# ScalarE takes the logarithms first, an affine step behind each, in the fractal stage of a four-layer kernel

## Chip, cores, metric

One core of a Trainium2 chip. The metric is the time of one launch on the device in microseconds. TensorE (PE in the profile, its weight loads PEld), VectorE (DVE), ScalarE (ACT), GpSimd (POOL) and SyncE (SP), which here issues DMAs, each run a queue of their own in order, and wait for one another through semaphores.

## What is computed

x has shape (16, 224, 224, 32) in fp32. Four layers follow each other, each of the form `x = x + f(group_norm(x))`; the change touches the first of them, the fractal layer:

```python
def _L0_conv_ref(x, gamma, beta, moving_mean, moving_var):
    x = sample_min_max_scaling(x)                       # (x - min) / (max - min + 1e-7), by sample
    measures = jnp.stack([box_sum(x, r) for r in (2, 4, 8, 16)], axis=-1)
    log_scales = jnp.log(jnp.asarray(SCALES))
    log_measures = jnp.log(measures + 1e-7)
    dls = log_scales - mean(log_scales)
    alphas = sum((log_measures - mean(log_measures)) * dls) / sum(dls ** 2)
    return (alphas - moving_mean) / jnp.sqrt(moving_var + 1e-3) * gamma + beta
x = x + _L0_conv_ref(_gn(x), ...)
```

box_sum(x, r) sums each channel over r x r pixels, stride 1, same size. The slope alpha of four logarithms is a fixed combination of them; with the batch-norm constants it becomes one scale and one bias for each channel. The other three layers (two spectral ones and a 7 x 7 convolution) are not touched.

## The kernel before

The program runs its layers as passes, one after the other, a barrier between them: `pass_fractal`, `mix_modes`, `pass_spectral`, `pass_conv`, `mix_modes`, `pass_inverse`. The change lies in `pass_fractal`, the first 3.6 ms. It goes through B = 16 samples. A sample has UN = 16 steps u: eight groups of four channels (cg) by two overlapping tiles of 128 rows (t). A step's tile is 128 rows by 224 columns by 4 channels.

What happens to step u of sample s, by engine:

- ScalarE `scale` (L350) applies the sample's normalisation and min-max scaling, from X into H0, in two halves. For u = 0 it waits for the sample's coefficients (`coef_ready`, from L673 on VectorE).
- VectorE `sums` (L526, L531, L534) adds H0 with itself shifted, in three levels, into Hb: sums over 2, 4 and 8 columns. The third sets h_ready, which frees H0 and starts the boxes.
- TensorE `boxes` (L429) multiplies these with band matrices: the sums over rows. It does so in four parts j, two for each half of the columns, each part with two PSUM banks. Parts 0 and 2 share their banks, as do 1 and 3, so part j waits for the logarithm of part j - 2 (ln_done), and sets m_ready.
- ScalarE `logs` (L361) takes the logarithm of each part, from PSUM into L (L[:, u % 2], four slots, one for each scale).
- VectorE `combine` (L541, L543) makes the slope out of the four slots, in L's slot 0 (t_ready). It waits for all four logarithms.
- ScalarE `affine` (L369) applies scale and bias, one instruction for each channel, from slot 0 into slot 2 of L (z_ready).
- VectorE `add` (L551) adds x and slot 2 into the compact buffer X1[:, u % 4] (x1_ready). It also waits until the buffer is free: the row matmuls (zps_ready) and the put-back (x_back) of four steps before.
- ScalarE `put_back` (L376) copies X1 into X, so that whole rows can be stored (x_back). VectorE `stats_of_x1` (L558) takes its group statistics. TensorE `over_rows` (L440) and `over_columns` (L451) transform X1 for the next layer, and ScalarE `keep_rows_done` (L381) moves the rows' result out of PSUM.

The order on each engine is written out by hand in its `body(prev, cur, nxt)`, which goes over the sixteen steps of one sample and mixes in what is left of the sample before and what prepares the next. For an ordinary step u:

- VectorE: sums(u+1) with stats_of_x1(u-2) between the levels, combine(u), add(u-1). In steps 4 to 10 then two or three pieces of statistics and extremes of the next sample (`stats_of_x`, L572 and L574), in step 11 their fold, in steps 3, 5, 6 and 12 to 14 small operations that make coefficients.
- ScalarE: scale(u+1), [keep_rows of prev in steps 1 and 2], put_back(u-2), [keep_rows in odd steps from 5], logs(u), affine(u-1). In step 15 it is scale of the next sample's step 0.
- TensorE: boxes(u), small matmuls of the statistics, [over_columns in steps 0, 3, 8, 12], over_rows. Step 1 has two over_rows, step 2 none.
- SyncE `finish`: when the last put-back of a sample is done (in ScalarE's step 1 of the next one), it stores the sample from X in two halves (L283), and when a half is stored it loads the same half of the sample after next into its place (L277). VectorE's first stats_of_x, in step 4, waits for the first half.

Two samples stand in one turn of a hardware loop (`Fori`); the first sample and the last are written out beside it.

Of the kernel before, what the change touches and what calls it, by code (L numbers as in the profile page):

```python
# [21 lines left out]
ALU = mybir.AluOpType  # L22
ACT = mybir.ActivationFunctionType
# [3 lines left out]
W = 224  # L27
# [7 lines left out]
HALF = W // 2  # L35
CG = 4
NCG = C // CG
# [40 lines left out]
def after(engine, sem, count):  # L78

    if not isinstance(count, int) or count > 0:  # L80
        engine.wait_ge(sem, count)
# [119 lines left out]
def pass_fractal(nc, B, d, keep):  # L201

    UN = NCG * T
    with Scope(nc, "a_") as z:
        X = z.sb("X", [P, 2, T, W, C])
        H0 = z.sb("H0", [P, WP, CG])
        Hb = z.sb("H", [P, 2, 3, WP, CG])
        L = z.sb("L", [P, 2, len(SCALES), W, CG])
        X1 = z.sb("X1", [P, 4, W, CG])
# [9 lines left out]
        eps = z.sb("eps", [P, 1])  # L219
        par4 = z.sb("par4", [P, 4, C])  # L220
        alp = z.sb("alp", [P, 2, C])
# [12 lines left out]
        PS = z.ps("PS", [P, 8, 512])  # L234
# [6 lines left out]
        sem = {n: z.sem(n) for n in names}  # L241
# [4 lines left out]
        def U(s, u):  # L246
            return s.e * UN + u
# [7 lines left out]
        def looped(engine, body, steps=None, per_turn=0):  # L255
            n = turns(body)
            with engine.Fori(0, n) as i:
                if steps:
                    steps.enter(i, per_turn)
                body(Sample(i, 0), Sample(i, 1), Sample(i, 2))  # L260
                body(Sample(i, 1), Sample(i, 2), Sample(i, 3))
            if steps:
                steps.leave(n)
            body(Sample(n, 0), Sample(n, 1), None)
            body(Sample(n, 1), None, None)
# [73 lines left out]
        @block.scalar  # L339
        def _(act):  # L340
            def scale(s, u):
                cg, t = divmod(u, T)
                if u == 0:
                    after(act, sem["coef_ready"], s.e + 1)
                    for j in range(T):
                        after(act, x_in[s.par][j], s.use * 16 + 16)
                after(act, sem["h_ready"], U(s, u))
                for k in range(0, CG, 2):
                    c = cg * CG + k
                    last = act.activation(H0[:, PAD:PAD + W, k:k + 2], X[:, s.par, t, :, c:c + 2], ACT.Relu,  # L350
                                          scale=cf[:, s.par, 0, c:c + 1], bias=cf[:, s.par, 1, c:c + 1])
                last.then_inc(sem["xs_ready"], 1)

            def logs(s, u):
                after(act, sem["x1_ready"], U(s, u) - 1)
                for j in range(4):
                    yh, sp_ = divmod(j, 2)
                    after(act, sem["m_ready"], U(s, u) * 4 + (j + 1))
                    out = L[:, u % 2, 2 * sp_:2 * sp_ + 2, HALF * yh:HALF * yh + HALF, :].rearrange("p s y c -> p s (y c)")
                    b0 = 2 * (j % 2)  # L360
                    act.activation(out, PS[:, b0:b0 + 2, 0:2 * W], ACT.Ln, bias=eps[:, 0:1])\  # L361
                       .then_inc(sem["ln_done"], 1)

            def affine(s, u):
                cg = u // T
                after(act, sem["t_ready"], U(s, u) + 1)
                for k in range(CG):
                    c = cg * CG + k
                    last = act.activation(L[:, u % 2, 2, :, k], L[:, u % 2, 0, :, k], ACT.Identity,  # L369
                                          scale=alp[:, 0, c:c + 1], bias=alp[:, 1, c:c + 1])  # L370
                last.then_inc(sem["z_ready"], 1)

            def put_back(s, u):
                cg, t = divmod(u, T)
                after(act, sem["x1_ready"], U(s, u) + 1)
                act.activation(X[:, s.par, t, :, cg * CG:cg * CG + CG], X1[:, u % 4], ACT.Copy)                   .then_inc(sem["x_back"], 1)  # L376

            def keep_rows_done(s, cg):
                after(act, sem["modes_ready"], s.e * 4 + (cg // 2 - 1))
                after(act, sem["zps_ready"], s.e * NCG + (cg + 1))  # L380
                act.activation(Zs[:, cg // 2 % 2, :, cg % 2, :], PS[0:YQ * CG, 4 + cg % 2, :].rearrange("p (y q) -> p y q", q=64),  # L381
                               ACT.Copy).then_inc(sem["zev_done"], 1)

            def body(prev, cur, nxt):
                for u in range(UN):
                    if u < UN - 1:
                        if cur:
                            scale(cur, u + 1)
                    elif nxt:
                        scale(nxt, 0)  # L390
                    if u == 0 and prev:
                        affine(prev, UN - 1)
                    if prev and u == 1:
                        keep_rows_done(prev, 6)
                    if prev and u == 2:
                        keep_rows_done(prev, 7)
                    if prev and u == 6:
                        after(act, sem["modes_ready"], prev.e * 4 + 4)
                        after(act, sem["modes_stored"], prev.e * 32 + 32)
                        act.activation(SO[:], PS[:, 6, :], ACT.Copy).then_inc(sem["modes_out"], 1)  # L400
                    if cur and u >= 2:
                        put_back(cur, u - 2)
                    elif prev and u < 2:
                        put_back(prev, UN - 2 + u)
                    if cur and u >= 5 and u % 2 == 1:
                        keep_rows_done(cur, (u - 5) // 2)
                    if cur:
                        logs(cur, u)
                    if u > 0 and cur:
                        affine(cur, u - 1)  # L410

            act.wait_ge(sem["setup"], 2)
            looped(act, body)

        @block.tensor
# [84 lines left out]
        def _(dve):  # L500
# [45 lines left out]
            def add(s, u):  # L546
                cg, t = divmod(u, T)
                after(dve, sem["z_ready"], U(s, u) + 1)
                after(dve, sem["zps_ready"], s.e * NCG + (u // 2 - 1))
                after(dve, sem["x_back"], U(s, u) - 3)  # L550
                dve.tensor_tensor(X1[:, u % 4], X[:, s.par, t, :, cg * CG:cg * CG + CG], L[:, u % 2, 2], ALU.add).then_inc(sem["x1_ready"], 1)  # L551

            def stats_of_x1(s, u, j):
                cg, t = divmod(u, T)
# [47 lines left out]
            def body(prev, cur, nxt):  # L602
                for u in range(UN):
# [43 lines left out]
                    if u > 0 and cur:  # L647
                        add(cur, u - 1)
                    if u == 0 and prev:
                        add(prev, UN - 1)  # L650
# [963 lines left out]
```

## Time and profile before

| | us |
|---|---|
| median of 3 runs | 8881.9 (8867.0 to 8884.9) |
| profiled execution | 8875.9 |
| its span, first to last instruction | 8874.3 |
| fractal stage within it | 0 to about 3620 |
| busy: TensorE, VectorE, ScalarE | 7419, 5668, 3869 |

The page divides the span into forty slices of 222 us; the digits are tenths. The first sixteen slices are the fractal stage, where the line of VectorE reads 7 to 8, that of TensorE 7 to 8, and that of ScalarE 6:

```profile
PE   5788777777877778579999997999999999429887
DVE  7888888888888887435544455555555554464444
ACT  4666666666666667213323332434434433101111
```

In a line of the groups, the name after the line number is the engine, then operation, what it writes and reads, shapes and count; behind the bar busy time, the mean of one in ns, and the idle time of the engine just before it with what ended it. In a timeline the first two numbers are the start in us from the span's start and the time taken; neighbours on one engine overlap by about 0.1 us, so the distance between starts is the better measure of what an instruction costs. A number in brackets is idle time just before it.

### The profile page before, as it was taken

Reading aid. Unit: us, or ns where it says so; the run is one execution under the profiler, and the core shown is the slowest. Engines: PE = TensorE matmul, PEld = TensorE weight load, DVE = VectorE, ACT = ScalarE, POOL = GpSimd, SP = SyncE. Lnnn points to the kernel's source line nnn. Section 1 sums busy time; section 2 is a strip of 40 time slices with the busy share of each in tenths; the row PEclk is TensorE's granted clock in tenths of the full one; section 3 lists DMA queues with packets and bytes.
Section 4 is the critical chain, followed back from the end, with each engine's and each line's share of the span. In section 5 each row is a group of like instructions: output and inputs, shape, how many; then the busy total and the mean of one; then the engine's idle time right before and its main releaser. Section 6 shows DMA issues by size and latency. Waiting matters only on the chain. (4 is left out here: it accounts for less than half of the span.)

```text
span 8874.3 us, 105845 instructions
## 1 busy us (share of the span) xinstructions
PE 7419.2 (84%) x34656; PEld 4519.8 (51%) x34656; DVE 5667.7 (64%) x10505; ACT 3869.1 (44%) x5030; POOL 276.2 (3%) x146
## 2 busy tenths in 40 slices
PE   5788777777877778579999997999999999429887
PEld 2444444444444444346666664566666666425444
DVE  7888888888888887435544455555555554464444
ACT  4666666666666667213323332434434433101111
POOL 0000000000000000100000000000000000000000
PEclk9989999999999999678888888999999999669998
DMA  1111111111111110644444445766766765589998
GB/s 71 64 64 64 64 64 64 64 64 64 64 64 64 64 64 31 173 115 138 150 130 136 136 136 174 180 168 167 183 166 165 181 170 150 185 300 241 262 256 237
DMA packets 780381, 1175.10 MB, mean 132 GB/s; under 512 B 154850, under 2 KB 693842, under 8 KB 759618
## 3 DMA queue, kind: packets, MB, share of 16 engines
q1 hardware_dynamic: 641858, 920.90, 34.9%
q10 hardware_dynamic: 133120, 140.54, 6.0%
q0 software_dynamic: 5120, 110.11, 3.9%
q8 instruction: 151, 2.47, 0.1%
q14 instruction: 132, 1.08, 0.0%
HBM read 706.47 MB, written 464.91 MB: 132 GB/s over the span
## 5 line engine op out<-in xcount | busy, mean ns | idle before, releaser
L429 PE MATMUL a_PS<-a_H,a_band 128*128 128x448 f32 x5120 | 2270.6, 596 | 656.1 <-ACT a_L L361 390.8
L429 PEld LDWEIGHTS a_PS<-a_H,a_band 128*128 128x128 f32 x5120 | 1027.9, 209 | 1739.1 <-issue 1146.3
L1163 PE MATMUL d_PS<-d_N,d_Bd 128*128 128x504 f32 x3072 | 1374.3, 599 | 85.6 <-ACT d_R L1270 58.1
L361 ACT ACTIVATE a_L<-a_PS,a_eps 128x896 f32<-128x896 f32 x1024 | 1007.3, 1003 | 666.1 <-PE a_PS L429 664.8
L1026 DVE SCALAR_TENSOR_TENSOR c_XO<-c_PS,c_XC 128x128 f32<-128x128 f32 x1792 | 495.9, 397 | 749.5 <-PE c_PS L948 746.1
L1163 PEld LDWEIGHTS d_PS<-d_N,d_Bd 128*128 128x128 f32 x3072 | 576.8, 193 | 739.6 <-issue 733.6
L1346 DVE TENSOR_TENSOR d_X<-d_R,d_X 128x504 f32<-128x504 f32 x512 | 348.3, 680 | 877.6 <-ACT d_R L1270 877.6
L541 DVE TENSOR_TENSOR a_L<-a_L 128x1792 f32<-128x1792 f32 x256 | 517.8, 2023 | 454.5 <-ACT a_L L361 454.5
L369 ACT ACTIVATE a_L<-a_L,a_alp 128x224 f32<-128x224 f32 x1024 | 732.6, 795 | 0.4 <-DVE a_L L543 0.4
L1469 DVE TENSOR_TENSOR e_OUT<-e_PS,e_X 112x224 f32<-112x224 f32 x1024 | 424.6, 531 | 455.7 <-PE e_PS L1424 254.3
L982 ACT ACTIVATE c_XT<-c_PS 128x512 f32<-128x512 f32 x448 | 267.5, 597 | 990.6 <-PE c_PS L937 990.5
L1270 ACT ACTIVATE d_R<-d_PS,d_b 128x504 f32<-128x504 f32 x512 | 346.7, 680 | 779.5 <-PE d_PS L1163 669.5
L948 PEld LDWEIGHTS c_PS<-c_Ws,c_XT 128*128 128x128 f32 x3584 | 457.1, 200 | 363.8 <-ACT c_XT L982 308.0
L1424 PE MATMUL e_PS<-e_V,e_G 128*112 128x448 f32 x1024 | 487.2, 604 | 85.6 <-DVE e_OUT L1469 85.6
L948 PE MATMUL c_PS<-c_Ws,c_XT 128*128 128x128 f32 x3584 | 545.5, 298 | 0.0
L1173 PEld LDWEIGHTS d_PS<-d_F,d_XP 112*112 112x112 f32 x4096 | 486.3, 184 | 96.8 <-issue 57.7
L944 PE MATMUL c_PS<-c_V,c_G 64*128 64x512 f32 x896 | 535.3, 679 | 0.2 <-DVE c_XO L1026 0.2
L1173 PE MATMUL d_PS<-d_F,d_XP 112*112 112x128 f32 x4096 | 491.4, 280 | 37.6 <-ACT d_XP L1230 37.6
L1303 DVE TENSOR_SCALAR d_N<-d_X,d_cf 128x56 f32<-128x56 f32 (+1 forms) x1536 | 482.9, 374 | 19.0 <-DMA d_X<-tmp_x 11.2
L572 DVE TENSOR_TENSOR a_run<-a_run,a_X 128x896 f32<-128x896 f32 x448 | 466.3, 1083 | 0.0
L440 PEld LDWEIGHTS a_PS<-a_F,a_X 128*112 128x112 f32 x4096 | 438.7, 180 | 51.9 <-issue 48.0
L1450 ACT ACTIVATE e_V<-e_PS 128x448 f32<-128x448 f32 x256 | 139.1, 543 | 735.4 <-PE e_PS L1415 735.4
(183 smaller groups left out, 8584.3 us busy)
## 6 DMA issues: line engine op xcount, KB each, us to landing
d_X<-tmp_x SPq DMA_DIRECT2D x512, 252.0 KB, 5.0
a_X<-in_x SPq DMA_DIRECT2D x32, 3584.0 KB, 19.0
c_XC<-tmp_x SPq DMA_DIRECT2D x448, 256.0 KB, 2.8
tmp_x<-d_X SPq DMA_DIRECT2D x512, 204.8 KB
tmp_x<-a_X SPq DMA_DIRECT2D x32, 3136.0 KB, 17.9
tmp_x<-c_XO SPq DMA_DIRECT2D x32, 3136.0 KB, 20.0
d_XR<-tmp_x ACTq DMA_DIRECT2D x256, 392.0 KB, 5.6
e_X<-tmp_x SPq DMA_DIRECT2D x256, 392.0 KB, 7.2
```

Source lines behind the costliest of these rows:

```text
L361: act.activation(out, PS[:, b0:b0 + 2, 0:2 * W], ACT.Ln, bias=eps[:, 0:1])\
L369: last = act.activation(L[:, u % 2, 2, :, k], L[:, u % 2, 0, :, k], ACT.Identity, scale=alp[:, 0, c:c + 1], bias=alp[:, 1, c:c + 1])
L429: last = pe.matmul(PS[:, 2 * (j % 2) + k, 0:2 * W], band[:, pos, :], Hb[:, u % 2, level, y1:y1 + HALF, :].rearrange("p y c -> p (y c)"), s ...
L541: steps.done(dve.tensor_tensor(lu[:, 0:2], lu[:, 0:2], lu[:, 2:4], ALU.subtract))
L572: steps.done(dve.tensor_tensor(run[:, j], first if k == 1 else run[:, j], now, op))
L944: pe.matmul(PS[:, 4 + n % 2, :], Gr[:, t, :], V[:, 16 * q:16 * q + 16, :].rearrange("a y c -> a (y c)"), start=True, stop=False)
L948: last = pe.matmul(PS[:, 4 + n % 2, j * P:j * P + P], XT[:, n % 2, j * P:j * P + P], Ws[:], start=False, stop=(j == 3))
L1026: last = dve.scalar_tensor_tensor(out=XO[:, t, ph, :, 4 * q:4 * q + 4].rearrange("p c y -> p y c"), in0=PS[:, 4 + n % 2, :].rearrange("p ( ...
L1163: last = pe.matmul(PS[:, c % 2, 0:NW], Bd[:, c * 3 + s, :], N2[:, c % 4, :, s:s + NY], start=(s == 0), stop=(s == 2))
L1173: last = pe.matmul(PS[0:HALF, 2 + 2 * (cg % 2) + yc, k * P:k * P + P], XP[:, cg % 2, k, t, 2 * yc:2 * yc + 2, :].rearrange("p k y -> p (k ...
L1303: last = dve.tensor_scalar(N2[:, c % 4, b0:b1, 1:1 + NY], X2[:, cg % 4, b0:b1, k, :], cf[:, v, 0, c:c + 1], cf[:, v, 1, c:c + 1], ALU.mult ...
L1424: last = pe.matmul(PS[0:R, 4 + 2 * (cp % 2) + t, 0:2 * W], Gr[:, t, :], V[:, cp % 4, :], start=True, stop=True)
```

## The change

In ScalarE's body the four logarithms of step u and the four affine instructions of step u-1 alternate, and stand right behind scale(u+1); keep_rows and put_back(u-2) come behind them. The affine writes into X1 in place of L's slot 2, and VectorE's add adds x to X1 in place. The waits that guard X1 (zps_ready, x_back) go from the add to the first affine, and the first logarithm waits for z_ready of two steps before (L read) where it waited for x1_ready of two steps before.

```diff
-            def logs(s, u):
-                after(act, sem["x1_ready"], U(s, u) - 1)
-                for j in range(4):
...
+            def logs(s, u, j):
+                if j == 0:
+                    after(act, sem["z_ready"], U(s, u) - 1)
+                yh, sp_ = divmod(j, 2)
+                after(act, sem["m_ready"], U(s, u) * 4 + (j + 1))
...
+            def affine(s, u, k):
                 cg = u // T
-                after(act, sem["t_ready"], U(s, u) + 1)
-                for k in range(CG):
-                    c = cg * CG + k
-                    last = act.activation(L[:, u % 2, 2, :, k], L[:, u % 2, 0, :, k], ACT.Identity,
-                                          scale=alp[:, 0, c:c + 1], bias=alp[:, 1, c:c + 1])
-                last.then_inc(sem["z_ready"], 1)
+                if k == 0:
+                    after(act, sem["t_ready"], U(s, u) + 1)
+                    after(act, sem["zps_ready"], s.e * NCG + (u // 2 - 1))
+                    after(act, sem["x_back"], U(s, u) - 3)
+                c = cg * CG + k
+                last = act.activation(X1[:, u % 4, :, k], L[:, u % 2, 0, :, k], ACT.Identity,
+                                      scale=alp[:, 0, c:c + 1], bias=alp[:, 1, c:c + 1])
+                if k == CG - 1:
+                    last.then_inc(sem["z_ready"], 1)
...
-                    if u == 0 and prev:
-                        affine(prev, UN - 1)
+                    for j in range(4):
+                        if cur:
+                            logs(cur, u, j)
+                        if u > 0 and cur:
+                            affine(cur, u - 1, j)
+                        elif u == 0 and prev:
+                            affine(prev, UN - 1, j)
...
+                    if cur and u >= 5 and u % 2 == 1:
+                        keep_rows_done(cur, (u - 5) // 2)
                     if cur and u >= 2:
                         put_back(cur, u - 2)
                     elif prev and u < 2:
                         put_back(prev, UN - 2 + u)
-                    if cur and u >= 5 and u % 2 == 1:
-                        keep_rows_done(cur, (u - 5) // 2)
-                    if cur:
-                        logs(cur, u)
-                    if u > 0 and cur:
-                        affine(cur, u - 1)
...
             def add(s, u):
                 cg, t = divmod(u, T)
                 after(dve, sem["z_ready"], U(s, u) + 1)
-                after(dve, sem["zps_ready"], s.e * NCG + (u // 2 - 1))
-                after(dve, sem["x_back"], U(s, u) - 3)
-                dve.tensor_tensor(X1[:, u % 4], X[:, s.par, t, :, cg * CG:cg * CG + CG], L[:, u % 2, 2], ALU.add).then_inc(sem["x1_ready"], 1)
+                dve.tensor_tensor(X1[:, u % 4], X1[:, u % 4], X[:, s.par, t, :, cg * CG:cg * CG + CG], ALU.add)\
+                   .then_inc(sem["x1_ready"], 1)
```

## Rows read from the trace of the kernel before

**Rows 1.** Groups by line from 0 to 3620 us, VectorE's, then ScalarE's.
```profile
L541 DVE TENSOR_TENSOR a_L<-a_L 128x1792 f32<-128x1792 f32 x256 | 517.8, 2023 | 454.5 <-ACT a_L L361 454.5
...
L543 DVE SCALAR_TENSOR_TENSOR a_L<-a_L 128x896 f32<-128x896 f32 x256 | 279.6, 1092 | 8.8
L551 DVE TENSOR_TENSOR a_X<-a_X,a_L 128x896 f32<-128x896 f32 x256 | 277.6, 1084 | 0.7 <-ACT a_L L369 0.7
...
L361 ACT ACTIVATE a_L<-a_PS,a_eps 128x896 f32<-128x896 f32 x1024 | 1007.3, 1003 | 666.1 <-PE a_PS L429 664.8 <-issue 0.2
...
L361 ACT ACT_TABLE_LOAD x1 | 1.3, 1283 | 0.0
```

**Rows 2.** VectorE's timeline: starts of L541, steps 0 to 4, 11 to 15, 0.
```profile
1422.14 2.03 DVE L541 TENSOR_TENSOR a_L<-a_L 128x1792 f32<-128x1792 f32 x1 [7.65 <-ACT a_L L361]
...
1433.33 2.03 DVE L541 TENSOR_TENSOR a_L<-a_L 128x1792 f32<-128x1792 f32 x1 [2.53 <-ACT a_L L361]
...
1444.80 2.03 DVE L541 TENSOR_TENSOR a_L<-a_L 128x1792 f32<-128x1792 f32 x1 [2.92 <-ACT a_L L361]
...
1457.38 2.02 DVE L541 TENSOR_TENSOR a_L<-a_L 128x1792 f32<-128x1792 f32 x1 [3.21 <-ACT a_L L361]
...
1468.72 2.03 DVE L541 TENSOR_TENSOR a_L<-a_L 128x1792 f32<-128x1792 f32 x1 [2.56 <-ACT a_L L361]
...
1578.02 2.01 DVE L541 TENSOR_TENSOR a_L<-a_L 128x1792 f32<-128x1792 f32 x1
...
1589.20 2.02 DVE L541 TENSOR_TENSOR a_L<-a_L 128x1792 f32<-128x1792 f32 x1 [1.43 <-ACT a_L L361]
...
1600.87 2.02 DVE L541 TENSOR_TENSOR a_L<-a_L 128x1792 f32<-128x1792 f32 x1 [0.77 <-ACT a_L L361]
...
1612.06 2.03 DVE L541 TENSOR_TENSOR a_L<-a_L 128x1792 f32<-128x1792 f32 x1 [2.33 <-ACT a_L L361]
...
1627.92 2.02 DVE L541 TENSOR_TENSOR a_L<-a_L 128x1792 f32<-128x1792 f32 x1 [4.45 <-ACT a_L L361]
...
1641.62 2.03 DVE L541 TENSOR_TENSOR a_L<-a_L 128x1792 f32<-128x1792 f32 x1 [3.11 <-ACT a_L L361]
```

**Rows 3.** ScalarE's timeline: step 2, and the scale of step 15.
```profile
1435.98 1.47 ACT L350 ACTIVATE a_H<-a_X,a_cf 128x448 f32<-128x448 f32 x2
...
1437.81 0.94 ACT L376 ACTIVATE a_X<-a_X 128x896 f32<-128x896 f32 x1
1438.65 1.89 ACT L361 ACTIVATE a_L<-a_PS,a_eps 128x896 f32<-128x896 f32 x2
...
1443.76 1.01 ACT L361 ACTIVATE a_L<-a_PS,a_eps 128x896 f32<-128x896 f32 x1 [0.50 <-PE a_PS L429]
1444.67 2.88 ACT L369 ACTIVATE a_L<-a_L,a_alp 128x224 f32<-128x224 f32 x4
...
1617.60 1.45 ACT L350 ACTIVATE a_H<-a_X,a_cf 128x448 f32<-128x448 f32 x2 [2.77 <-DVE a_cf L673]
```

**Rows 4.** TensorE's timeline: steps 0 (second half), 1 and 2.
```profile
1414.56 6.51 PE L429 MATMUL a_PS<-a_H,a_band 128*128 128x448 f32 x10 [4.34 <-ACT a_L L361]
...
1424.22 8.03 PE L429 MATMUL a_PS<-a_H,a_band 128*128 128x448 f32 x20
1432.09 3.27 PE L440 MATMUL a_PS<-a_F,a_X 128*112 128x64 f32 x32
...
1439.70 4.03 PE L429 MATMUL a_PS<-a_H,a_band 128*128 128x448 f32 x10 [0.52 <-ACT a_L L361]
```

**Rows 5.** Windows: stretch, length, busy time of each engine, granted clock, DMA share, GB/s.
```profile
1416.00:1420.00 4.00, 4.00 (x7) 1.88 (x6) 0.00 (x0) 0.56 (x1) 0.00 (x0) 0.55 0.00 0
```

**Rows 6.** SyncE's timeline, and the time to landing by DMA issue, 1400 to 1640 us.
```profile
1427.45 0.91 SPq L283 DMA_DIRECT2D tmp_x<-a_X  x2
1441.26 9.05 SPq L277 DMA_DIRECT2D a_X<-in_x  x2
...
a_X<-in_x SPq DMA_DIRECT2D x2, 3584.0 KB, 18.2
```

More of the change, by code:

```diff
@@ L352, in scale @@
                 last.then_inc(sem["xs_ready"], 1)
-            def logs(s, u):
-                after(act, sem["x1_ready"], U(s, u) - 1)
-                for j in range(4):
[L357 to L364, printed above, removed]
-                cg = u // T
-                after(act, sem["t_ready"], U(s, u) + 1)
-                for k in range(CG):
-                    c = cg * CG + k
-                    last = act.activation(L[:, u % 2, 2, :, k], L[:, u % 2, 0, :, k], ACT.Identity,
-                                          scale=alp[:, 0, c:c + 1], bias=alp[:, 1, c:c + 1])
-                last.then_inc(sem["z_ready"], 1)
+            def logs(s, u, j):
[3 more added lines that the diff above has]
+                after(act, sem["m_ready"], U(s, u) * 4 + (j + 1))
+                out = L[:, u % 2, 2 * sp_:2 * sp_ + 2, HALF * yh:HALF * yh + HALF, :].rearrange("p s y c -> p s (y c)")
+                b0 = 2 * (j % 2)
+                act.activation(out, PS[:, b0:b0 + 2, 0:2 * W], ACT.Ln, bias=eps[:, 0:1]).then_inc(sem["ln_done"], 1)
+            def affine(s, u, k):
+                cg = u // T
+                if k == 0:
[7 more added lines that the diff above has]
+                    last.then_inc(sem["z_ready"], 1)
             def put_back(s, u):
```

## Prediction

> **What bounds the kernel now.** I read the page's forty slices first: in the fractal stage, the first 3.6 ms, VectorE's line is the fullest, and neither it nor TensorE's is full. So I asked the groups by line for the stretch where VectorE's idle time is. It sits in front of one instruction, the first subtraction of `combine` (L541): 454.5 us over 256 steps, each time released by ScalarE's logarithms (L361) [rows 1]. That is the most that any reordering on ScalarE can give back.
>
> Then I listed the starts of L541 through one whole sample; call them c(0) to c(15), one for each step u of 16 [rows 2]. The distance between two of them is one step. Steps 4 to 11, in which VectorE also takes the next sample's statistics, need 1578.02 - 1468.72 = 109.3 us for seven and show no idle: VectorE's own. The other nine have idle time before L541: 2.53, 2.92, 3.21, 2.56, 1.43, 0.77, 2.33, 4.45 and 7.65 or 3.11 us [rows 2].
>
> What ScalarE does in that idle time is in its timeline of step 2 [rows 3], TensorE's beside it [rows 4]. ScalarE: scale, keep_rows, put_back, two logarithms back to back, a wait for TensorE, two more, then the four affines. The put-back has to wait for VectorE's add, the first logarithm stands behind it, and TensorE's second half of the boxes (j = 2, 3) waits for that logarithm, because it reuses its banks: the wait "<-ACT a_L L361" of 0.52 us [rows 4]. The loop of an ordinary step is therefore combine 3.07 and add 1.0 (2.02, 1.09 and 1.08, of which neighbours overlap by some 0.1 [rows 1]), put_back 0.84, first logarithm to the matmul that it frees 1.05, second half of the boxes to the last logarithm 4.06 (1439.70 to 1443.76), logarithm 1.04: 11.1 us, with 0.47 for keep_rows (1435.98 to 1437.81 less the scale's 1.36) in some steps 11.5. The trace has 11.19 and 11.47. So the loop is understood, and the add and the put-back are in it without need.
>
> **The change part by part.** Per step it removes nothing and adds no instruction: four logarithms, four affines, one put-back, one add before and after.
>
> (a) The affine writes into X1, and the add works in place there. L is then free as soon as the affine has read it, so the logarithms no longer wait for the add of two steps before. The wait on z_ready in their place names affines that stand earlier on ScalarE itself: nothing. Strides and sizes of the affine stay; the add reads one compact and one strided tile as before. I take zero; the add's 1.0 is the only term that could move.
>
> (b) The waits for zps_ready and x_back move from VectorE's add to ScalarE's first affine. The rows matmul asked for stands on TensorE before the boxes whose logarithm precedes that affine, and x_back is ScalarE's own. Both are met on arrival: zero. Were it late, three logarithms and, behind them, TensorE's j = 3 would be held.
>
> (c) The put-back goes behind the logarithms: 0.84 us and the 1.0 of the add leave the loop.
>
> (d) The affines go between the logarithms. The first needs t_ready, that is combine's end, c + 3.1; the other three logarithms are queued behind it. New loop: 3.18 + affine 0.70 + logarithm 0.90, then either TensorE's j = 3 (1.5) plus 0.2, or ScalarE's own affine, logarithm, affine (2.3), then 1.04: about 8.1 us. In steps 4 to 11 that stands against 15.6 on the mean, so nothing is lost there even if the j = 3 matmuls run at half clock.
>
> With the loop at 8.1, three other things are late next, all near 9.5. VectorE's work of a step is distance less idle, 8.5 to 8.8 in ordinary steps, 9.37 in 2 to 3, 9.75 in 11 to 12, 10.9 in 12 to 13 [rows 2]. ScalarE's work in order is the last affine 0.70, put_back 0.84, scale 1.36, then four logarithms at 0.90 with three affines at 0.70 between: 8.7 to 9.2, with keep_rows the more [rows 3]. TensorE's second half may start only once the first logarithm has run. That starts at c + 3.2 after a keep_rows (0.7 + 0.47 + 0.84 + 1.36, less 0.14 by which ScalarE is free before c), and with 1.05, 4.06 plus 0.1 for an affine in the way, and 1.04 the next c is 9.5 later, without keep_rows 9.0. TensorE's work is boxes 7.87 (1424.22 to 1432.09) plus rows 1.55 (half of 3.27 less the overlap), 9.4 [rows 4]; in the four steps a sample with columns matmuls it ran without idle in 11.19, so these two are 3.3.
>
> So step by step, before and after, in us:
> 15 to 0: two forms that alternate. With the idle of 7.65 it is 16.1, after 9.5. Where the hardware loop turns it is 13.70, of which 3.11 are idle, so VectorE needs 10.6 there, 2.1 over the other form; after 10.9. Mean gain 4.7.
> 0 to 1: 11.19, TensorE already runs through (3.3 + 7.87): 0.
> 1 to 2: 11.47, after 7.87 + 3.1 = 11.0: 0.5.
> 2 to 3: 12.58, after 9.5: 3.1.
> 3 to 4: 11.34, TensorE again: 0.
> 4 to 11: 109.3, VectorE: 0.
> 11 to 12: 11.18 to 9.75: 1.4.
> 12 to 13: 11.67 to 10.9: 0.8.
> 13 to 14: 11.19 to 8.9: 2.3.
> 14 to 15: 15.86; here ScalarE waits at scale for the next sample's coefficients, and starts at 1617.60, 5.5 after c(14) [rows 3]. Scale 1.4, logarithm 1.05, second half at low clock 5.7 (between the 4.03 and the 6.51 below), logarithm 1.04 give 14.8; only put_back and keep_rows leave: 1.1.
> Sum 13.9 a sample. Fourteen samples have this form: 195. The first starts with larger idle and has no earlier one; by the same steps I estimate 20. The last takes no statistics, so its steps 4 to 11 are ordinary too: nine at about 1.8, two with columns at 0.3, and the 4 us of steps 1 to 3 as above, 21. Together 236 us.
>
> The clock: the second half of the boxes took 4.03 us in one step and 6.51 in another, after 4.34 us without work [rows 4]; in that stretch the granted clock was 0.55 [rows 5], so it was for most of it at the lower of its levels, 1.2 GHz. The gaps that the change closes are of this kind, so I count these steps at full clock, except 14 to 15, where a gap of 3.8 us remains.
>
> (e) The put-back of step 15 is also what the sample's store waits for, on SyncE's queue, and behind the store stands the load of the sample after next. It is issued at 1427.45, 5.3 after c(0); the load's first half is issued at 1441.26 and takes 18.2 us by the median, so it lands 32 us after the store's issue [rows 6], 13 us before it is wanted. VectorE wants it at c(4) + 4.1, here 1472.8. After the change the put-back is the last thing of step 1: c(1) + 2.0 = c(0) + 13.2, 8 us later, and c(4) comes 3.5 us earlier. Landing at c(0) + 45.5, wanted at c(0) + 47.2. The cover shrinks to 1.7 us. I count zero, but a faster start than mine can't show in steps 0 to 4, and each us of delay beyond it would cost 14.
>
> **The sum.** The profiled execution took 8875.9 us (span 8874.3 and 1.6 around it): 8876 - 236 = 8640. The median of the runs shown is 6 us above it: 8646 us.
>
> **The rivals.** First, *function changes cost time.* All activations of this stage now alternate Ln and Identity: seven changes between the two in a step, where now there is one. The stage shows one table load at L361, 1283 ns, in 1024 logarithms [rows 1], although each step already goes from Relu and Copy to Ln and to Identity; and from logarithm to affine it is 0.91 us (1443.76 to 1444.67), as from logarithm to logarithm [rows 3]. That speaks against it. If each change did load, a step would take 8.7 + 7 x 1.28 = 17.7 us on ScalarE, 256 of them 4530 against 3510 (16 x 219.5): about 9900 us. It decides, against the forecast, from some 0.25 us a change, where six more changes use up the nine steps' gain of 1.5 us each. 3%. The Trainium skill has a rule that speaks against this change, in ScalarE: Activation LUTs, section "Table sets: the hidden batching unit": "Batch activation calls by **set**, not by function." Taken as batching by function it would give this rival's result; the same section of the Trainium skill says that the cheap functions, identity among them, are in every set, and by that it would cost nothing; with this the trace agrees (0.91 us, no load between).
>
> Second, *the overlap of neighbours on ScalarE is lost.* A logarithm lasts 1.01 but the next starts after 0.90. If each waiting instruction lost this 0.1, the path through a step grows by up to 0.8: 0.8 in the three steps that ScalarE sets, 0.2 in the others, 3 us a sample, and 10 in the last: 8700 us. For it: every logarithm has a wait of its own. Against: two logarithms whose waits were met ran 1.89 together. 15%.
>
> Third, *the load lands late or the clock stays low.* 3 us late in every sample is 42 us: 8688. One second half at low clock in each sample costs 1.4 to 2.5 us, 20 to 35: 8675. 17%.
>
> Fourth, *nothing is gained*, since TensorE sets more steps than I see; for it, its share in steps 0 to 1 and 3 to 4; against, its idle time behind L361. 8876, 4%.
>
> **How the numbers follow.** Forecast 8646 (8610 to 8670), 59%; the rest as above, with 2% for something slower that I don't see. Range 8600 to 8735: below, 14 to 15 at full clock (22 us) and a little more; above, the second and third rival together. About 0.2% (18 us) is what a measurement of this kernel can tell from no change. Faster 0.91, same 0.04, slower 0.05.
>
> **What would show it.** c(2) to c(3) near 9.5, c(13) to c(14) near 8.9, c(15) to c(0) near 9.5 and 10.9, c(0) to c(1) and c(4) to c(11) as they are. VectorE's idle before L541 falls from 454 to some 210 us. The store goes out about 13 us after c(0). No idle before the first statistics of X; if there is, its mean is the third rival's price. Wrong would be: idle time or a load between a logarithm and its affine; steps 4 to 11 over 109.3, which would mean that the logarithms are held behind the first affine.

## The result, and the profile after

The changed kernel takes 8671.5 us (median of 4 runs) against 8883.4 (median of 4): a ratio of 0.976, 95% interval 0.975 to 0.978. Its profiled execution has a span of 8670.7 us, 204 less than before. The forecast was 8646 in a range of 8600 to 8735.

The groups by line from 0 to 3620 us, VectorE's and then ScalarE's, answer to [rows 1]; L541, L543 and L551 are now L544, L546 and L552, the boxes L432, the rows L443, the affine L370, the put-back L378:

```profile
L544 DVE TENSOR_TENSOR a_L<-a_L 128x1792 f32<-128x1792 f32 x256 | 517.3, 2021 | 242.7 <-ACT a_L L361 241.0
...
L576 DVE BATCH_NORM_STATS2 a_sx_bn<-a_X 128x6 f32<-128x448 f32 x512 | 293.5, 615 | 2.7 <-DMA a_X<-in_x 2.4
...
L552 DVE TENSOR_TENSOR a_X<-a_X 128x896 f32<-128x896 f32 x256 | 277.6, 1084 | 0.7 <-ACT a_X L370 0.7
...
L361 ACT ACTIVATE a_L<-a_PS,a_eps 128x896 f32<-128x896 f32 x1024 | 1024.4, 1000 | 594.9 <-PE a_PS L432 594.0
```

VectorE's instructions last as long as they did, the add in place too (1084 ns both times). Its idle time before the first subtraction went from 454.5 to 242.7 us: 212 of the 221 us by which the stage's last c(15) comes earlier.

The starts of that subtraction in one sample, steps 0 to 4, 11 to 14, as in [rows 2]:

```profile
717.69 2.02 DVE L544 TENSOR_TENSOR a_L<-a_L 128x1792 f32<-128x1792 f32 x1 [0.83 <-ACT a_L L361]
728.57 2.02 DVE L544 TENSOR_TENSOR a_L<-a_L 128x1792 f32<-128x1792 f32 x1 [2.22 <-ACT a_L L361]
739.25 2.03 DVE L544 TENSOR_TENSOR a_L<-a_L 128x1792 f32<-128x1792 f32 x1 [2.33 <-ACT a_L L361]
748.72 2.02 DVE L544 TENSOR_TENSOR a_L<-a_L 128x1792 f32<-128x1792 f32 x1
760.04 2.03 DVE L544 TENSOR_TENSOR a_L<-a_L 128x1792 f32<-128x1792 f32 x1 [2.55 <-ACT a_L L361]
...
869.51 2.02 DVE L544 TENSOR_TENSOR a_L<-a_L 128x1792 f32<-128x1792 f32 x1
878.78 2.02 DVE L544 TENSOR_TENSOR a_L<-a_L 128x1792 f32<-128x1792 f32 x1
889.61 2.02 DVE L544 TENSOR_TENSOR a_L<-a_L 128x1792 f32<-128x1792 f32 x1
902.24 2.02 DVE L544 TENSOR_TENSOR a_L<-a_L 128x1792 f32<-128x1792 f32 x1 [3.78 <-ACT a_L L361]
```

Step 2 to 3 is 9.47 us, step 4 to 11 is 109.47. I took the same distances over all of both traces; the means of the fourteen inner samples stand beside the forecast's, in us:

| step | before, mean | forecast | after, mean |
|---|---|---|---|
| 15 to 0 | 15.1 | 10.2 | 10.1 |
| 0 to 1 | 11.2 | 11.2 | 10.9 |
| 1 to 2 | 11.5 | 11.0 | 10.7 |
| 2 to 3 | 12.2 | 9.5 | 9.5 |
| 3 to 4 | 11.3 | 11.3 | 11.3 |
| 4 to 11 | 109.3 | 109.3 | 109.6 |
| 11 to 12 | 11.4 | 9.75 | 9.3 |
| 12 to 13 | 11.7 | 10.9 | 10.9 |
| 13 to 14 | 11.2 | 8.9 | **12.3** |
| 14 to 15 | 16.0 | 14.8 | 14.3 |
| sample | 220.9 | 207 | 208.7 |

One step has gone the wrong way: 13 to 14.

### The profile page after: what moved, and what is told of

Read it like the earlier page. It is cut to its first block and busy times, and to the rows that moved or that the text cites. A ratio compares the mean times of both kernels' runs of the same rounds, so it can differ in the third digit from the quotient of the medians.

```text
span 8670.7 us, 105831 instructions
## 1 busy us (share of the span) xinstructions
PE 7411.1 (85%) x34656; PEld 4564.0 (53%) x34656; DVE 5662.7 (65%) x10505; ACT 3838.0 (44%) x5030; POOL 276.3 (3%) x146
## 5 line engine op out<-in xcount | busy, mean ns | idle before, releaser
L432 PE MATMUL a_PS<-a_H,a_band 128*128 128x448 f32 x5120 | 2230.0, 594 | 397.6 <-DVE a_H L537 319.4
L432 PEld LDWEIGHTS a_PS<-a_H,a_band 128*128 128x128 f32 x5120 | 1046.0, 210 | 1422.9 <-issue 1217.7
L370 ACT ACTIVATE a_X<-a_L,a_alp 128x224 f32<-128x224 f32 x1024 | 816.2, 797 | 6.7 <-DVE a_L L546 6.7
L544 DVE TENSOR_TENSOR a_L<-a_L 128x1792 f32<-128x1792 f32 x256 | 517.3, 2021 | 242.7 <-ACT a_L L361 241.0
L350 ACT ACTIVATE a_H<-a_X,a_cf 128x448 f32<-128x448 f32 x512 | 380.6, 799 | 362.4 <-DVE a_H L537 296.9
L443 PEld LDWEIGHTS a_PS<-a_F,a_X 128*112 128x112 f32 x4096 | 457.3, 187 | 51.2 <-issue 48.2
L443 PE MATMUL a_PS<-a_F,a_X 128*112 128x64 f32 x4096 | 464.2, 270 | 2.4 <-DVE a_X L552 2.4
```

Source lines behind the costliest of these rows:

```text
L370: last = act.activation(X1[:, u % 4, :, k], L[:, u % 2, 0, :, k], ACT.Identity, scale=alp[:, 0, c:c + 1], bias=alp[:, 1, c:c + 1])
L432: last = pe.matmul(PS[:, 2 * (j % 2) + k, 0:2 * W], band[:, pos, :], Hb[:, u % 2, level, y1:y1 + HALF, :].rearrange("p y c -> p (y c)"), s ...
L443: last = pe.matmul(PS[0:YQ * CG, 4 + cg % 2, yq * 64:yq * 64 + 64], X1[:, (2 * cg + t) % 4, yq * YQ:yq * YQ + YQ, :].rearrange("p y c -> p ...
L544: steps.done(dve.tensor_tensor(lu[:, 0:2], lu[:, 0:2], lu[:, 2:4], ALU.subtract))
```

## The experiments

**The compact buffer alone.** The old order, but the affine writes into X1 and the add works in place.

```diff
...
-                    last = act.activation(L[:, u % 2, 2, :, k], L[:, u % 2, 0, :, k], ACT.Identity,
+                    last = act.activation(X1[:, u % 4, :, k], L[:, u % 2, 0, :, k], ACT.Identity,
...
```

> The kernel before, with one part of the change alone: the affine writes into X1 and the add works in place; ScalarE's order stays (put_back, four logarithms, four affines). My theory: the loop combine, add, put_back, first logarithm is unchanged, because the put-back waits for the add whatever the affine writes into. Ordinary steps stay at 11.19 and 11.47, time 8883 (within 5). A rival, that writing into the compact buffer frees L and that this is the gain, gives the 8671 of the changed kernel.

Measured: 8890.5 us, ratio 1.0007 (0.9997 to 1.0016). The first steps of a sample, by the starts of the first subtraction (here L543):

```profile
1425.50 2.02 DVE L543 TENSOR_TENSOR a_L<-a_L 128x1792 f32<-128x1792 f32 x1 [7.62 <-ACT a_L L361]
1436.69 2.02 DVE L543 TENSOR_TENSOR a_L<-a_L 128x1792 f32<-128x1792 f32 x1 [2.50 <-ACT a_L L361]
1448.17 2.03 DVE L543 TENSOR_TENSOR a_L<-a_L 128x1792 f32<-128x1792 f32 x1 [2.93 <-ACT a_L L361]
```

11.19 and 11.48 us, as in [rows 2]. The buffer alone is worth nothing.

**The order alone.** The new order; the affine writes into L's slot 2 as before, so the first logarithm of a step waits for the add of two steps before.

```diff
-                    after(act, sem["z_ready"], U(s, u) - 1)
+                    after(act, sem["x1_ready"], U(s, u) - 1)
...
```

> The changed kernel with its new order on ScalarE, but the affine writes into slot 2 of L as before, so the first logarithm of a step waits for the add of two steps before. My theory: that add ends 4.18 us after c, where the first logarithm would start at 3.2; so a step that ScalarE and TensorE set goes from 9.5 to 10.4: c(2) to c(3), c(11) to c(12), half of c(15) to c(0), some 2.8 us a sample and 8 in the last: 8720. If the order alone carried all of it, 8671. If the buffer carried it, 8883.

Measured: 8743.0 us, ratio 0.984 (0.982 to 0.985). ScalarE's timeline in a step of the last sample shows the wait:

```profile
3384.46 1.49 ACT L350 ACTIVATE a_H<-a_X,a_cf 128x448 f32<-128x448 f32 x2
3387.26 1.01 ACT L361 ACTIVATE a_L<-a_PS,a_eps 128x896 f32<-128x896 f32 x1 [1.31 <-DVE a_X L552]
3388.16 0.81 ACT L368 ACTIVATE a_L<-a_L,a_alp 128x224 f32<-128x224 f32 x1
3388.85 1.00 ACT L361 ACTIVATE a_L<-a_PS,a_eps 128x896 f32<-128x896 f32 x1
```

The logarithm starts at 3387.26, 4.19 us after the first subtraction at 3383.07 (the forecast had 4.18), and the step is 10.42 us. Two thirds of the gain are there; some 72 us hang on this one wait. It came 23 us above my 8720. The largest part is step 2 to 3: in eleven of the fourteen inner samples it took 12.1 to 12.2 us instead of 10.5, some 18 us in all. TensorE waits 2.3 us there for the first logarithm, and in one of those samples the second half of the boxes behind this wait took 5.72 us, at a granted clock of 0.50 from 756 to 758 us; I had counted the step at full clock.

**The order alone, with the wait one logarithm later.** Slot 2 is first written by the second logarithm of a step, so that is where the wait has to stand.

```diff
+                if j == 1:
+                    after(act, sem["x1_ready"], U(s, u) - 1)
...
```

> As order_only (new order, affine into slot 2 of L), but the wait for the add of two steps before stands at the second logarithm of a step, the first that writes slot 2, and not at the first. The add is done 4.18 us after c, the second logarithm is due at 4.4 to 4.9, after an affine that waits for combine. My theory: the wait is met and nothing of order_only's 1.0 us a step remains: steps at 9.5, 8671 as with the compact buffer. If it is the buffer that pays, 8743 as order_only.

Measured: 8666.9 us, ratio 0.976 (0.974 to 0.977): the changed kernel's time, without its buffer. So the gain is the order. What the compact buffer does is to take away a wait, and only if that wait stands at the first logarithm.

**The affines behind, not between.** The changed kernel with all four logarithms ahead of the four affines.

```diff
                     for j in range(4):
                         if cur:
                             logs(cur, u, j)
+                    for j in range(4):
                         if u > 0 and cur:
                             affine(cur, u - 1, j)
```

> The changed kernel (logarithms ahead of the put-back, X1 as target), but the four affines stand behind all four logarithms instead of one behind each. My theory: the next step's first logarithm then stands behind 2.77 of affines, 0.84 put_back, 1.36 scale, so it starts at c + 4.8 instead of 3.2 or less, and ordinary steps take 11.0 to 11.5, as in the kernel before; what stays is the gain at 15 to 0 and at 14 to 15, some 4.5 us a sample: 8815. If only the order against the put-back mattered, 8671.

Measured: 8799.0 us, ratio 0.990 (0.989 to 0.992). ScalarE in the last sample:

```profile
3408.38 2.89 ACT L370 ACTIVATE a_X<-a_L,a_alp 128x224 f32<-128x224 f32 x4
3411.16 0.57 ACT L383 ACTIVATE a_Zs<-a_PS 112x512 f32<-112x512 f32 x1
3411.64 0.93 ACT L378 ACTIVATE a_X<-a_X 128x896 f32<-128x896 f32 x1
3412.48 1.44 ACT L350 ACTIVATE a_H<-a_X,a_cf 128x448 f32<-128x448 f32 x2
3413.81 1.88 ACT L361 ACTIVATE a_L<-a_PS,a_eps 128x896 f32<-128x896 f32 x2
3417.41 1.01 ACT L361 ACTIVATE a_L<-a_PS,a_eps 128x896 f32<-128x896 f32 x1 [1.72 <-PE a_PS L433]
```

From the affines at 3408.38 to the logarithm at 3413.81 are 5.43 us in which TensorE's second half can't start. Of the last sample's steps from 4 to 14 those without columns matmuls take 10.98, 11.44 or 13.1 us, where the changed kernel takes 9.1 to 9.9. The put-back is behind the logarithms here as well; without the affines between them that gives back only 84 of 212 us. Not all of it is where I had expected it: 11 to 12 and 12 to 13 keep the changed kernel's 9.3 and 10.8 us and 15 to 0 takes 12.3 on the mean, but 2 to 3 and 13 to 14 take 13.0 and 12.8, more than in the kernel before.

**The step that got slower.** TensorE's timeline of the changed kernel in steps 13 and 14, and the windows of the same stretch (length, busy time of TensorE, its weight loads, VectorE, ScalarE, GpSimd, granted clock):

```profile
880.33 7.74 PE L432 MATMUL a_PS<-a_H,a_band 128*128 128x448 f32 x20
889.75 0.38 PE L480 MATMUL a_PS<-a_ident,a_nm 128*2 128x128 f32 x2 [1.68 <-DVE a_nm L602]
890.06 1.96 PE L443 MATMUL a_PS<-a_F,a_X 128*112 128x64 f32 x16
891.81 9.29 PE L432 MATMUL a_PS<-a_H,a_band 128*128 128x448 f32 x20
```

```profile
888.00:892.00 4.00, 2.32 (x20) 2.03 (x20) 3.76 (x12) 4.00 (x7) 0.00 (x0) 0.94 0.00 0
892.00:896.00 4.00, 4.00 (x8) 1.86 (x8) 3.96 (x7) 0.66 (x2) 0.00 (x0) 0.63 0.00 2
```

TensorE is through with the boxes of step 13 and waits 1.68 us for nm, the extremes of the next sample, with the rows matmuls and the next boxes queued behind. Then the granted clock is 0.63, partly the lower level of 1.2 GHz, and the boxes take 9.29 us instead of 7.74. The experiment lets the rows matmuls go ahead of this one:

```diff
-                    if nxt and u == 13:
-                        after(pe, sem["sx_in"], nxt.e * 4 + 3)
-                        pe.matmul(STX[0:2, 64:64 + P], nm[:], ident[:], start=True, stop=True)\
-                          .then_inc(sem["sx_out"], 1)
...
                     if cur and u >= 3:
                         over_rows(cur, (u - 3) // 2, (u - 3) % 2)
+                    if nxt and u == 13:
+                        after(pe, sem["sx_in"], nxt.e * 4 + 3)
+                        pe.matmul(STX[0:2, 64:64 + P], nm[:], ident[:], start=True, stop=True)\
+                          .then_inc(sem["sx_out"], 1)
```

> The changed kernel with one move on TensorE: in step 13 the small transposing matmul of the statistics, which waits for VectorE's nm, stands behind the rows matmuls instead of ahead of them. In the changed kernel TensorE waits 1.68 us for it with rows and the next boxes queued behind, and c(13) to c(14) took 12.3 on the mean against my 8.9. Theory one, this wait costs its 1.6 us and lets the clock fall on top: step 13 to 14 falls to between 8.9 and 10.7, 25 to 45 us in all, 8635. Theory two, the clock falls there for what came before, whatever this wait: the step stays above 12 and the time within 10 us of 8671.

Measured: 8631.6 us, ratio 0.972 (0.970 to 0.973), 40 us below the changed kernel. The same place:

```profile
877.21 1.69 PE L443 MATMUL a_PS<-a_F,a_X 128*112 128x64 f32 x16
878.84 0.38 PE L495 MATMUL a_PS<-a_ident,a_nm 128*2 128x128 f32 x2
879.15 7.78 PE L432 MATMUL a_PS<-a_H,a_band 128*128 128x448 f32 x20
```

No wait, and the boxes take 7.78 us. Step 13 to 14 fell from 12.33 to 9.46 us on the mean, and theory one holds. Step 14 to 15 rose from 14.3 to 15.0. TensorE waits 3.4 us in it in both kernels, but the second half of its boxes behind that wait does not always take the same time. The same sample in the changed kernel, then in this one:

```profile
910.30 4.03 PE L432 MATMUL a_PS<-a_H,a_band 128*128 128x448 f32 x10 [3.37 <-ACT a_L L361]
```

```profile
896.15 6.85 PE L432 MATMUL a_PS<-a_H,a_band 128*128 128x448 f32 x10 [3.38 <-ACT a_L L361]
```

The step's own values in the changed kernel part the two costs of the wait for nm. In six of the fourteen inner samples TensorE waited 0.98 to 1.42 us, the next boxes took 7.74 and the step 10.6 to 11.0 (10.85 on the mean): the wait alone. In the other eight it waited 1.54 to 2.22 us, the boxes took 8.9 to 10.0 and the step 12.6 to 14.3: wait and clock.

**The store one step later.** The changed kernel's loads land just when VectorE wants them, so I moved them back by one step more, to see what a us beyond the cover costs.

```diff
...
-                    elif prev and u < 2:
-                        put_back(prev, UN - 2 + u)
+                    if prev and u == 0:
+                        put_back(prev, UN - 2)
+                    if prev and u == 2:
+                        put_back(prev, UN - 1)
...
```

> The changed kernel with the put-back of step 15 moved one step further back, into step 2 of the next sample. My theory that the store and the load behind it have used up their cover (loads now land 0.1 us ahead of or 0.3 us behind the statistics that want them): the store goes out at c(0) + 23.6 instead of 13.0, the load lands 33.3 later, VectorE wants it at c(0) + 46.4, so it waits some 10 us in front of the first statistics in each of 14 samples: 8815. If there were cover left, or if VectorE's wait were made good later in the sample, 8671 to 8700.

Measured: 8816.2 us, ratio 0.992 (0.991 to 0.994). VectorE's timeline from c(4) on, and the group over the stage:

```profile
995.36 2.02 DVE L548 TENSOR_TENSOR a_L<-a_L 128x1792 f32<-128x1792 f32 x1 [2.55 <-ACT a_L L361]
...
1009.07 1.15 DVE L580 BATCH_NORM_STATS2 a_sx_bn<-a_X 128x6 f32<-128x448 f32 x2 [9.56 <-DMA a_X<-in_x]
```

```profile
L580 DVE BATCH_NORM_STATS2 a_sx_bn<-a_X 128x6 f32<-128x448 f32 x512 | 293.4, 615 | 122.7 <-DMA a_X<-in_x 122.7
```

One put-back of 0.95 us, moved by one step, costs 145 us: 122.7 of it stand in front of the statistics, and step 2 to 3, which holds one more put-back now, takes 11.35 instead of 9.5.

**The coefficients earlier.** rows_first, and on VectorE the small operations that end in the next sample's coefficients stand ahead of combine(14) instead of behind add(13).

```diff
+                    if nxt and u == 14:
+                        after(dve, sem["sx_out"], nxt.e * 4 + 4)
...
                     if cur:
                         combine(cur, u)
                     if u > 0 and cur:
                         add(cur, u - 1)
...
-                    if nxt and u == 14:
-                        after(dve, sem["sx_out"], nxt.e * 4 + 4)
```

> rows_first with one more move, on VectorE: in step 14 the small operations that make the next sample's coefficients stand ahead of combine(14) instead of behind add(13). TensorE's part of them is ready 1.2 us before c(14), and VectorE is idle there. My theory that step 14 to 15 is the chain coefficients, scale, logarithm, boxes: the coefficients come some 5 us earlier, the scale is no longer late, and the step falls from 14.97 to 9.5 or 10, 75 us in all: 8555. If the low clock after a gap of other origin sets the step, it stays above 13 and the gain is under 25 us.

Measured: 8555.2 us, ratio 0.963 (0.961 to 0.964). VectorE around c(14) and c(15):

```profile
872.45 0.15 DVE L650 COPY a_rng<-a_PS 128x2 f32<-128x2 f32 x1
...
873.50 0.30 DVE L660 TENSOR_SCALAR a_cf<-a_sx_ab,a_rng 128x32 f32<-128x32 f32 x1
873.71 2.02 DVE L544 TENSOR_TENSOR a_L<-a_L 128x1792 f32<-128x1792 f32 x1
...
882.67 2.02 DVE L544 TENSOR_TENSOR a_L<-a_L 128x1792 f32<-128x1792 f32 x1 [0.61 <-ACT a_L L361]
```

The coefficients are there by c(14); in rows_first the scale that waits for them started some 5.5 us after it. Step 14 to 15 is 8.96 here, 9.03 on the mean instead of 14.97; step 13 to 14 pays 0.6 for it. The low clock in this step was a consequence: all twenty matmuls of the boxes now run without a pause and in 7.74 us, in each of the fourteen inner samples.

```profile
873.77 7.74 PE L432 MATMUL a_PS<-a_H,a_band 128*128 128x448 f32 x20
```

**And the store back to its early place.** coef_early with put_back(prev, UN - 1) ahead of step 1's logarithms.

```diff
+                    if prev and u == 1:
+                        put_back(prev, UN - 1)
                     for j in range(4):
                         if cur:
                             logs(cur, u, j)
...
```

> coef_early with the put-back of step 15 ahead of step 1's logarithms again, where the kernel before had it. The add it waits for is done at c(0) + 4.2, the first logarithm of step 1 can start at 4.5 for TensorE's sake, so it delays no more than 0.5 us that TensorE's own 10.9 covers; the store goes out at c(0) + 5.3 and the load lands 7 us before it is wanted. My theory: step 4 to 5 is 14.0 in every sample (now 14.16 on the mean), no idle before the first statistics, 3 us in all: 8552. A rival, that the put-back in that place costs its 0.85 us in step 0 to 1, gives 8565.

Measured: 8554.4 us, ratio 0.963 (0.961 to 0.964): no difference from coef_early that can be measured. Both theories had a part: the idle time before the statistics fell from 2.8 to 0.8 us over the stage, and step 0 to 1 rose from 10.9 to 11.3.

## Why the prediction was right, and where it was not

The loop of combine, add, put-back, first logarithm and second half of the boxes was read rightly. Its parts were undone one by one. In the last sample, in the steps from 5 to 14 without columns matmuls, it takes 11.2 to 11.7 us before, 11.0 or 11.4 (and 13.1 in three of seven) with the put-back behind but the affines behind too, 10.4 with the affines between but the add's wait still at the first logarithm, and 9.1 to 9.5 with both gone.

(a) and (b), zero for the buffer and for the moved waits, hold: x1_only is within 0.2% of before, and order_wait1 has the whole gain without the buffer. In the trace of the changed kernel the affine's idle time is 6.7 us in all, for combine and never for zps_ready or x_back.

(c) and (d) hold: steps 4 to 11 did not suffer from the logarithms queued behind the first affine, 109.6 against 109.3, and the difference is in step 4 to 5. Part of it is the load; in every second sample 0.15 us are a pause among the small statistics operations, which x1_only has too.

What is late next was named rightly for nine of the ten kinds of step in the table, within about 0.5 us. In 15 to 0, 2 to 3, 3 to 4 and 12 to 13 the miss is 0.1 us or less. In 0 to 1 and 1 to 2 I took 7.87 for the boxes from [rows 4]; they run in 7.57 (926.95 to 934.52 in the trace of the changed kernel). The 0.3 us more was still a little of the wait for ScalarE: the first logarithm started 2.97 us after the boxes (1427.19 against 1424.22), in the changed kernel 2.51, and coef_early_store, with the put-back ahead of it again, takes 11.26 us. So what I called TensorE's own was not free of the cause that the change removes. In 11 to 12 the forecast's 9.75 was 0.5 too much: VectorE runs through the step in 9.27, and in the kernel before it had a pause of 0.33 us ahead of its sums (at 1583.45) that I counted as work.

The step that failed is 13 to 14. I counted the small matmul of the statistics there at its own 0.36 us and took the rows and the next boxes as free to start once TensorE was. It has a wait of its own, for VectorE's nm, and VectorE is the slower of the two in step 13. In the kernel before, TensorE came to it almost as late as nm did and waited 0.36 us. The result was 12.3 instead of 8.9: 3.4 us in each inner sample, 48 in fourteen. rows_first took 40 of them away in this step and lost 10 again in 14 to 15; its last c(15) comes 34 us earlier, and its measured time is 40 lower. The other terms were a little better than forecast, 1.7 us a sample, 24, so the inner samples gave 171 us instead of 195; the first gave 17 instead of 20 and the last 36 instead of 21, and the stage's first c came 3 us later. For the last sample the forecast has no term for 15 to 0, which gained 6.6 us (16.1 to 9.5), and its nine ordinary steps gained 22 us instead of 16, 3.5 of it in 4 to 5 and 4.3 in 14 to 15. Had I counted these, the forecast would have been lower and further off: the misses partly cancel. Together the last c(15) went from 3586.88 to 3365.93, 221 us against the forecast's 236.

```profile
3365.93 2.02 DVE L544 TENSOR_TENSOR a_L<-a_L 128x1792 f32<-128x1792 f32 x1 [3.75 <-ACT a_L L361]
```

The span fell by 204 only, since the passes behind the stage, whose code is the same, took 17 us more in this execution: 5304.8 us from the last c(15) to the end of the span, 5287.4 before. In the traces of the eight experiments this rest is between 5288 and 5307 us with no relation to what was changed. Why it varies stays open. So the profiled execution misses its 8640 by 32 us, of which 15 are the stage and 17 are not.

The cover of the load, (e), was 1.7 us in the forecast and is none in the trace: four of the fourteen inner samples wait, 0.13 to 0.25 us in three and 1.44 in one. The store's issue and the load's in one sample:

```profile
1146.34 0.90 SPq L283 DMA_DIRECT2D tmp_x<-a_X  x2
1160.29 10.71 SPq L277 DMA_DIRECT2D a_X<-in_x  x2
```

It is issued 13.0 us after c(0) = 1133.30, as forecast. The size that was off is the way from the store's issue to the load's landing: I took 32 us from one sample of the kernel before, where it is 32.1, the shortest of its fourteen; the medians are 33.3 before and 33.4 after. So the load lands at c(0) + 46.4 by the median instead of 45.5, and it is wanted at c(0) + 46.4 instead of 47.2, since steps 0 to 2 came out shorter than forecast. All these waits together are 2 us.

Of the rivals, the first (function changes) is ruled out by the trace. ScalarE's timeline of the changed kernel in step 0:

```profile
931.05 1.00 ACT L361 ACTIVATE a_L<-a_PS,a_eps 128x896 f32<-128x896 f32 x1
931.95 0.82 ACT L370 ACTIVATE a_X<-a_L,a_alp 128x224 f32<-128x224 f32 x1
...
934.81 0.99 ACT L361 ACTIVATE a_L<-a_PS,a_eps 128x896 f32<-128x896 f32 x1
935.70 0.80 ACT L370 ACTIVATE a_X<-a_L,a_alp 128x224 f32<-128x224 f32 x1
936.38 0.59 ACT L383 ACTIVATE a_Zs<-a_PS 112x512 f32<-112x512 f32 x1
```

Logarithm to affine is 0.90 us, affine to the next function 0.68, no table load in between. With this the second rival falls too: the overlap of 0.1 us stays although each logarithm has a wait of its own. What "ScalarE: Activation LUTs" in the Trainium skill says under "Table sets: the hidden batching unit", that sets and not functions are what to batch by, fits this trace; that no set changes here is read from the absence of a load between the two, not from the sets themselves. The third rival's clock came true in part, in step 13 to 14, for a cause that I had not named there, and its late load in one sample of fourteen. The fourth (nothing is gained) is ruled out by the time.

## What to carry over

When an order of work on one engine holds up a loop over three engines, write the loop down with its durations, then take out what is in it without need, and ask of every small instruction on the engine that is freed what it waits for: its wait was hidden while that engine came late. Interleaving independent work (here one affine behind each logarithm) fills gaps that a producer leaves anyway: it brought 128 of the 212 us, on top of the 84 for moving the put-back out of the way. What it is worth with the put-back still ahead was not run. Count the cover of a transfer that hangs on what is moved back: 13 us were used up here, and one step more (11 us) cost 145.

## What was not expected of the hardware

A wait of 1.68 us of TensorE was followed by a stretch with a granted clock of 0.63 in which twenty matmuls took 9.29 us instead of 7.74; in eight of the fourteen inner samples the step was longer by such a stretch, in six not, with the same instructions. So the gap's price was nearly doubled. The step took 2.9 us more on the mean than in rows_first (12.33 against 9.46); the wait itself was 1.64 on the mean, and some 1.2 are left for the clock, an estimate. The waits were also longer in the eight than in the six (1.96 against 1.22 on the mean). Which samples get the low clock behind a wait is not explained: behind the same 3.4 us in step 15 it was there in some samples and not in others. The low clock behind the wait for the coefficients vanished with that wait.
